# A transformer tower on one core: the engines' hand-ordered lists laid out anew, and the constant table loaded in two parts

## The chip, the cores and the metric

The kernel runs on one core of a Trainium2 chip. The metric is device time in microseconds (us) of that core; lower is better. A core has TensorE (PE in the rows, its weight loads PEld), VectorE (DVE), ScalarE (ACT), GpSimd (POOL) and SyncE (SP), which here only issues loads. Each engine runs its own program in order; an instruction that waits for a semaphore holds everything behind it on that engine.

## The reference

128 images of 3 x 64 x 64 are cut into 16 patches each (16 x 16 x 3 = 768 numbers), embedded to 192, and a class token is put ahead: 17 tokens an image. Two layers follow.

```
h0 = patches @ W.T + b, class token first                     # 17 x 192 per image
layer 0: h1 = h0 + attention(layernorm(h0))                   # 12 heads of 64; lowest scores dropped, softmax
         h2 = h1 + quantised gated feed-forward(h1)           # 8-bit rows, ternary weights, hidden 512
layer 1: h3 = h2 + linear attention(h2)                       # 12 heads of 16, causal, each head normalised,
                                                              # gate from tanh and a cosine
         out = h3 + layernorm-ed feed-forward(h3)             # hidden 128
```

## The kernel before

Seven images (119 rows, `ROWS`) are a group; 18 full groups and one of two images (34 rows) make 19. Each group goes through five chains of short instructions: patches and embedding (banks `E0`, `E1`), softmax attention (`A0`, `A1`), the quantised feed-forward (`M0`, `M1`), linear attention (`L0`, `L1`, called `bank_lin`), and the last feed-forward. The groups are staggered: in one step of the loop the newest group is embedded while the one before does its scores, the next its probabilities, and so on, six deep (`DEPTH`).

The order of the work on each engine is written out by hand as three lists of (group, piece): `fill` for steps 0 to 7 with absolute groups, `steady` for the ten steps 8 to 17 (a hardware loop over five pairs of steps; the number is how many groups behind the newest), and `drain` for the rest. `program` (line 379) runs them. Pieces on TensorE begin with `t_`, on VectorE `v_`, on ScalarE `a_`, on GpSimd `p_`. All dependences are semaphores, counted by group; so a list changes what stands behind what, never what is computed.

The pieces that matter here, with their lines. `v_sq_sum` (1088) gives the sum of squares of each head, `p_rstd_h` (622; instructions at 521 and 522) raises it to the power -1/2, `v_att1` (1092) multiplies, `t_att1` (1960) transposes it (helper `turn`, line 1554, records all transposes), `a_att1_T` copies it out. `t_down` (1873) needs `int_outT` from `a_out_T` and gives `v_h2` (1018) its input. `t_dots` (1761) gives the scores that `v_pack` (831) packs; `t_dots1` needs the packs 0 and 1. `t_embed` (1669) needs both halves of `patchT`. `v_shifted` (892), `v_feat_q`, `v_feat_k` (1052) and `v_hidT` (1041) end VectorE's list of a step; `t_params`, `t_lin_first` (1934) stand behind them on TensorE. `v_quant_in` (974) leads to ScalarE's `a_int_in`, TensorE's `t_int_in`, `t_gate`, `t_up`; then `v_gated` (983), `v_product` (990), GpSimd's `p_scaled` (551). `v_v1` (1061) and the three `v_causal` (masking products, `weightsT`, line 916) are what `t_num` (the numerators, line 1948) waits for; `t_num_turn` and `v_centred` lead on to the next `v_sq_sum`.

`zero_products` (1559) multiplies zeros into an unused bank: work for TensorE with no result, put in where it would idle. At the start TensorE multiplies 12 of them, waits for the constants (`ld_const`) and the first weights (`ld_tok`), transposes `w_tok_raw`, multiplies the start rows (1583), and enters its list. `late_setup` (358), called `wait_late` in the lists, waits for the setup's last pieces: `ready` and six loads, two of which SP issues only after VectorE's `setup_biases`.

The constant table (128 x 642) holds the identity (columns 0 to 127), the mask factors, the token kinds, the block and causal masks and two parity columns.

## Time and profile before

| | us |
|---|---|
| median of 3 runs (644.97 to 650.62) | 645.59 |
| the profiled execution, its time | 645.34 |
| its span, first to last instruction | 643.4 |
| TensorE busy | 577.2 |
| VectorE busy | 455.9 |
| ScalarE busy | 317.7 |
| GpSimd busy | 305.1 |
| mean granted clock of TensorE | 0.962 |

A granted clock of 1.00 is 2.4 GHz, 0.50 is 1.2 GHz. The page of the profile gives busy times and the costliest groups of instructions; the trace behind it can be asked who waited for whom, what ran in order of time, and how busy each engine was in a stretch. A waiting time in square brackets in a row of the order of time is idle time of that engine just ahead of the instruction, with what ended it. Start times are from the start of the span.

### The profile page before, as it was taken

How to read it: one execution, taken by the hardware profiler on the slowest of the kernel's cores; microseconds unless marked ns; L12 is line 12 of the kernel's file. 1: busy time of each engine (PE TensorE's matmuls, PEld its weight loads, DVE VectorE, ACT ScalarE, POOL GpSimd, SP SyncE). 2: the span in 40 equal slices, each digit the busy share in tenths (PEclk: the TensorE clock that was granted, in tenths of full speed). 3: DMA queues.
4: the chain of work that ended last, by engine and by line, in shares of the span. 5: the costliest groups of instructions: out<-in, count | busy, mean ns of one | idle time of the engine just before them, and what ended most of it. 6: DMA issues, size and time to landing. Idle time of an engine off the chain costs nothing. (4 is left out here: it accounts for less than half of the span.)

```text
span 643.4 us, 15871 instructions
## 1 busy us (share of the span) xinstructions
PE 577.2 (90%) x5229; PEld 468.1 (73%) x5229; DVE 455.9 (71%) x2101; ACT 317.7 (49%) x849; POOL 305.1 (47%) x788
## 2 busy tenths in 40 slices
PE   7999998989998989889897979797989899988985
PEld 4677877878887877778786868786877777764542
DVE  0587686778868577768695969586868677877743
ACT  2253755628371727273746465454646373725410
POOL 1011155455553546363646465555545454656564
PEclk7999999989996989898999999899989999979999
DMA  9721000000000000000000000000000000000000
GB/s 227 180 63 45 2 23 5 21 2 28 23 9 5 24 7 23 7 21 6 21 13 14 27 0 27 0 27 0 12 0 6 0 7 1 3 2 13 7 1 13
DMA packets 11062, 14.69 MB, mean 23 GB/s; under 512 B 2160, under 2 KB 8657, under 8 KB 11017
## 3 DMA queue, kind: packets, MB, share of 16 engines
q1 hardware_dynamic: 8712, 12.44, 7.3%
q10 hardware_dynamic: 2304, 1.67, 0.9%
q8 instruction: 25, 0.41, 0.3%
q14 instruction: 21, 0.16, 0.1%
HBM read 12.44 MB, written 1.67 MB: 22 GB/s over the span
## 5 line engine op out<-in xcount | busy, mean ns | idle before, releaser
L521 POOL TENSOR_TENSOR spread<-moments,gain_eps 119x1 f32<-119x1 f32 x57 | 10.9, 191 | 104.1 <-DVE moments L801 104.1
L522 POOL TENSOR_TENSOR rstd<-spread,minus_half 119x1 f32<-119x1 f32 (+1 forms) x95 | 55.4, 583 | 7.5
L1729 PEld LDWEIGHTS bank_embed<-norm0T,w_qkv 128*128 128x128 f32 x456 | 55.9, 194 | 3.7 <-ACT norm0T L1328 1.0
L1729 PE MATMUL bank_embed<-norm0T,w_qkv 128*128 128x119 f32 (+1 forms) x456 | 58.0, 278 | 0.0
L565 POOL TENSOR_TENSOR feat_k<-feat_qk,consts 128x238 f32<-128x238 f32 (+1 forms) x38 | 21.9, 597 | 63.3 <-DVE feat_qk L1052 63.3
L1673 PE MATMUL bank_embed<-w_tok,patchT 128*119 128x192 f32 (+1 forms) x228 | 45.6, 354 | 0.0
L1302 ACT COPY norms2T<-bank_lin 96x476 f32<-96x476 f32 (+1 forms) x19 | 10.2, 537 | 69.7 <-PE bank_lin L1554 69.7
L522 POOL TENSOR_TENSOR rstd_h<-spread_h,minus_half 119x12 f32<-119x12 f32 x19 | 43.3, 2279 | 1.5
L1673 PEld LDWEIGHTS bank_embed<-w_tok,patchT 128*119 128x119 f32 (+1 forms) x228 | 39.5, 196 | 3.1 <-issue 1.3
L1346 ACT COPY qkT<-bank_embed 128x357 f32<-128x357 f32 (+1 forms) x76 | 32.0, 445 | 18.5 <-PE bank_embed L1738 18.5
L916 DVE TENSOR_TENSOR weightsT<-bank_lin,consts 119x476 f32<-119x476 f32 (+1 forms) x57 | 34.7, 626 | 9.1 <-PE bank_lin L1934 8.8
L1832 PE MATMUL bank_att<-w_o,att0T 128*119 128x192 f32 (+1 forms) x228 | 40.9, 328 | 0.0
L831 DVE TENSOR_REDUCE scores<-bank_att 119x51 f32<-119x357 f32 (+1 forms) x76 | 36.1, 499 | 5.7 <-PE bank_att L1784 5.4
L1910 PEld LDWEIGHTS bank_lin<-norms2T,w_qkv 97*128 97x128 f32 (+1 forms) x304 | 38.1, 200 | 2.0 <-ACT norms2T L1302 1.6
L1910 PE MATMUL bank_lin<-norms2T,w_qkv 97*128 97x119 f32 (+3 forms) x304 | 39.4, 285 | 0.0
L551 POOL TENSOR_TENSOR scaled<-product,g_out 119x512 f32<-119x512 f32 x19 | 24.4, 1282 | 31.3 <-DVE product L990 31.2
L1832 PEld LDWEIGHTS bank_att<-w_o,att0T 128*119 128x119 f32 (+1 forms) x228 | 35.6, 179 | 0.8 <-ACT att0T L1374 0.2
L1554 PE MATMUL bank_lin<-consts,att 119*96 119x119 f32 (+1 forms) x38 | 8.7, 316 | 30.6 <-DVE att L1092 30.6
L1361 ACT ACTIVATE wide<-probs,consts 119x68 f32<-119x68 f32 x133 | 35.1, 346 | 0.2 <-DVE probs L907 0.2
L1738 PE MATMUL bank_embed<-norm0T,w_qkv_rest 64*128 64x119 f32 (+1 forms) x456 | 35.1, 286 | 0.0
L871 DVE MATCH_REPLACE8 kept<-top,scores 119x20 f32<-119x20 f32 x228 | 34.5, 165 | 0.0
L1328 ACT COPY norm0T<-bank_embed 128x238 f32<-128x238 f32 (+1 forms) x19 | 6.6, 349 | 56.1 <-PE bank_embed L1554 56.1
(255 smaller groups left out, 1629.7 us busy)
## 6 DMA issues: line engine op xcount, KB each, us to landing
strips<-x SPq DMA_DIRECT2D x18, 336.0 KB
out<-result ACTq DMA_DIRECT2D x18, 89.2 KB
w_qkv<-L_attn_w_qkv SPq DMA_DIRECT2D x2, 576.0 KB, 7.9
w_in_raw<-L_ffn_w_in SPq DMA_DIRECT2D x1, 768.0 KB, 12.0
w_tok_raw<-L_tok_W SPq DMA_DIRECT2D x1, 576.0 KB
w_qkv_rest<-L_attn_w_qkv SPq DMA_DIRECT2D x2, 288.0 KB, 10.0
w_o<-L_attn_w_out SPq DMA_DIRECT2D x1, 576.0 KB
w_qkv_raw<-L_attn_Wqkv SPq DMA_DIRECT2D x1, 432.0 KB
```

Of the source, the lines that this page charges most:

```text
L522: pool.tensor_tensor(rstd_out, spread, minus_half[0:ROWS, 0:spread.shape[1]], ALU.pow) \
L551: pool.tensor_tensor(scaled[:, :], product[:, :], g_out[:, :], ALU.mult).then_inc(S["scaled"], 1)
L831: dve.tensor_reduce(scores[0:r, place:place + 3, TOKENS - 1::-1], parts(src, 3)[0:r, :, 0:r].rearrange("p h (b j) -> p h j b", j=TOKENS), ...
L871: last = dve.match_replace(kept[:, h, :], top[:, h, :], scores[:, h, :], BIG)
L916: dve.tensor_tensor(dst[0:r, :, 0:r], src[0:r, :, 0:r], mask[0:r, 0:r].unsqueeze(1).to_broadcast([r, 4, r]), ALU.mult).then_inc(ready_sem, 1)
L1346: act.copy(qkT[:, p, QTILES * n + 3 * s:QTILES * n + 3 * s + 3, 0:r], parts((E0, E1)[s], 3)[:, :, 0:r]) \
L1361: last = act.activation(wide[:, 8:12, b], probs[:, 8:12, :], ACT.Copy, scale=block_mask[:, b * TOKENS:b * TOKENS + 1])
L1673: last = pe.matmul(E0[0:r, 0:EMBED], patchT[:, k, 0:r], w_tok[:, k, :], start=k == 0, stop=k == CHUNKS - 1)
L1729: pe.matmul(parts((E0, E1)[s], 3)[:, j, 0:r], w_qkv0[:, tile * 128:(tile + 1) * 128], norm0T[:, s, 0:r], start=j == 0, stop=False, skip_gr ...
L1738: last = pe.matmul(parts((E0, E1)[s], 3)[:, j, 0:r], w_qkv0_rest[rows, n, j * 128:(j + 1) * 128], norm0T[rows, 1 - s, 0:r], start=False, s ...
L1832: last = pe.matmul(A1[0:r, 0:EMBED], att0T[:, t, 0:r], w_o0[:, t, :], start=t == 0, stop=t == QTILES - 1)
L1910: last = pe.matmul(parts(L1, 4)[:, j, 0:r], w_qkv1[0:rows, k, first:first + 128], norms2T[0:rows, 2 + k, 0:r], start=k == 0, stop=k == 1)
```

## The change

All twelve lists are laid out anew: `fill`, `steady` and `drain` of TensorE, VectorE, ScalarE and GpSimd. Every piece is still there once per group. The loads and waits at the start are changed as well:

```diff
-            load(ld_const, consts[:, :], table)
+            load(ld_tok, consts[:, 0:128], table[:, 0:128])
             load(ld_tok, w_tok_raw[:, :, :], a["L0_tok_W"].rearrange("(k p) n -> p k n", k=2))
             load(ld_tok, start_rows[0:1, :], row(a["L0_tok_b"]))
             load(ld_tok, start_rows[1:2, :], a["cls_tok"].rearrange("a b n -> (a b) n"))
             load_strips(0, 0)
+            load(ld_const, consts[:, 128:C_WIDTH], table[:, 128:C_WIDTH])
...
             dve.wait_ge(ld_const, 16)
+            dve.wait_ge(ld_tok, 64)
...
-            multiply_zeros(L1, 12)
-            pe.wait_ge(ld_const, 16)
-            pe.wait_ge(ld_tok, 48)
+            multiply_zeros(L1, 21)
+            pe.wait_ge(ld_tok, 64)
...
+            pe.wait_ge(ld_const, 16)
             pe.matmul(M1[0:ROWS, 0:EMBED], token_kind, start_rows[:, :], start=True, stop=True).then_inc(setup_pe, 1)
```

The `steady` lists, TensorE's whole and of the others the stretches that the prediction speaks of:

```diff
 # TensorE
-                (4, t_params), (5, t_hid1), (4, t_lin_first), (2, t_probs1), (3, t_int_in), (5, t_out4), (2, t_probs0), (4, t_lin_rest),
-                (3, t_gate), (1, t_k_main), (3, t_up), (2, t_probs2), (1, t_k_rest), (4, t_num), (2, t_att0_0), (2, t_att0_1),
-                (4, t_num_turn), (2, t_proj0_0), (2, t_proj0_1), (3, t_int_out), (0, t_patches1), (0, t_patches0), (4, t_att1),
-                (3, t_down), (1, t_dots0), (0, t_embed), (3, t_norms2), (1, t_dots1), (4, t_proj1), (3, t_qk1), (0, t_norm0), (3, t_hid),
-                (0, t_q_main), (4, t_norm3), (0, t_q_rest), (0, t_v0), (0, t_v1),
+                (4, t_params), (5, t_hid1), (4, t_lin_first), (3, t_int_in), (5, t_out4), (2, t_probs0), (3, t_up), (3, t_gate),
+                (1, t_k_main), (4, t_lin_rest), (2, t_probs2), (2, t_probs1), (1, t_k_rest), (4, t_num), (2, t_att0_0), (2, t_att0_1),
+                (4, t_num_turn), (2, t_proj0_0), (2, t_proj0_1), (3, t_int_out), (0, t_patches1), (0, t_patches0), (3, t_down),
+                (1, t_dots0), (0, t_embed), (4, t_att1), (3, t_norms2), (1, t_dots1), (4, t_proj1), (3, t_qk1), (0, t_norm0), (3, t_hid),
+                (0, t_q_main), (0, t_q_rest), (0, t_v0), (4, t_norm3), (0, t_v1),
 # VectorE
-                (4, v_causal1), (4, v_causal0), (5, v_out4), (4, v_causal2), (3, v_gated), (3, v_product), (4, v_v1), (3, v_umax_out),
...
-                (4, v_centred), (4, v_sq_sum), (2, v_h1), (4, v_att1), (2, v_stats1), (2, v_moments1), (2, v_u_in), (3, v_h2),
-                (3, v_stats2), (3, v_moments2), (1, v_pack1), (1, v_pack0), (3, v_norms2), (5, v_moments4), (1, v_top0), (0, v_h0),
...
-                (4, v_norm3), (1, v_drop1), (1, v_mix), (1, v_least), (3, v_feat_q), (1, v_shifted), (3, v_feat_k), (3, v_hidT),
+                (3, v_amax_in), (2, v_exp_sum), (3, v_unit_in), (3, v_quant_in), (2, v_exp_inv), (2, v_probs), (2, v_wide0),
+                (4, v_causal0), (5, v_out4), (5, v_stats4), (5, v_moments4), (2, v_wide1), (4, v_causal1), (3, v_gated), (3, v_product),
+                (4, v_v1), (4, v_causal2), (3, v_row_gain), (3, v_umax_out), (3, v_amax_out), (5, v_scaled4), (3, v_unit_out),
+                (3, v_quant_out), (4, v_num_sum), (4, v_den), (4, v_centred), (4, v_sq_sum), (2, v_h1), (2, v_stats1), (3, v_h2),
+                (3, v_stats2), (3, v_moments2), (2, v_moments1), (1, v_pack1), (1, v_pack0), (4, v_att1), (3, v_norms2), (1, v_top0),
...
+                (4, v_norm3), (1, v_drop0), (1, v_mix), (3, v_feat_q), (3, v_feat_k), (1, v_least), (3, v_hidT), (1, v_shifted),
 # ScalarE
-                (3, a_int_out), (1, a_k_0), (3, a_out_T), (0, a_patchT0), (4, a_att1_T), (0, a_patchT1), (3, a_norms_T), (0, a_norm0T),
+                (2, a_probsT1), (3, a_square), (0, a_strips), (4, a_num_T), (2, a_att0), (1, a_k_0), (2, a_att1), (3, a_big_out),
+                (3, a_int_out), (1, a_k_1), (3, a_out_T), (0, a_patchT0), (0, a_patchT1), (4, a_att1_T), (3, a_norms_T), (5, a_store),
 # GpSimd
-                (4, p_wave), (5, p_h3_beta), (4, p_terms), (1, p_h0), (4, p_series), (4, p_overlap), (3, p_scaled), (3, p_rms),
-                (4, p_centred_sq), (4, p_den_sq), (4, p_rstd_h), (2, p_rstd1), (3, p_rstd2), (5, p_rstd4), (0, p_rstd0), (4, p_rstd3),
+                (4, p_wave), (4, p_terms), (4, p_series), (4, p_overlap), (5, p_h3_beta), (3, p_scaled), (3, p_rms), (1, p_h0),
+                (4, p_den_sq), (4, p_centred_sq), (4, p_rstd_h), (3, p_rstd2), (5, p_rstd4), (2, p_rstd1), (0, p_rstd0), (4, p_rstd3),
```

In `fill` and `drain` the pieces stand in much the same order as in `steady`. `wait_late` is earlier in ScalarE's `fill` (behind `(1, a_probsT1)` instead of behind `(5, a_k_1)`), later on VectorE, TensorE and GpSimd. The zero products of TensorE's lists add up to 175 where there were 152 (without the 12, now 21, at the start); the largest group, ahead of `t_att1` of the last group of images, has 22 instead of 12.

## Rows read from the trace of the kernel before

**Rows 1.** The page, part 1: busy us (share of span) x instructions of each engine.

```profile
PE 577.2 (90%) x5229; PEld 468.1 (73%) x5229; DVE 455.9 (71%) x2101; ACT 317.7 (49%) x849; POOL 305.1 (47%) x788
```

**Rows 2.** Waits of TensorE, whole span: us in total, times, longest.

```profile
PE bank_lin L1554 <- DVE att L1092: 30.6, 16, 2.6
PE bank_lin L1948 <- DVE v L1061: 11.3, 9, 1.3
PE bank_att L1778 <- DVE scores L831: 4.5, 3, 2.3
```

**Rows 3.** First, 14th `att1` in order of time; then two steps' busy time, PEclk.

```profile
105.87 0.36 DVE L1092 TENSOR_TENSOR att<-centred,rstd_h 119x192 f32<-119x192 f32 x1 [1.04 <-POOL rstd_h L522]
...
506.00 0.36 DVE L1092 TENSOR_TENSOR att<-centred,rstd_h 119x192 f32<-119x192 f32 x1 [2.02 <-POOL rstd_h L522]
...
383.09:413.31 30.22, 26.64 (x263) 23.04 (x263) 23.23 (x108) 16.57 (x44) 16.02 (x40) 1.00 0.05 14
413.31:444.55 31.24, 27.89 (x263) 24.33 (x263) 23.47 (x109) 16.57 (x44) 15.97 (x40) 0.95 0.05 14
```

**Rows 4.** Busy time and granted clock of one us behind an `att1` wait.

```profile
415.00:416.00 1.00, 1.00 (x10) 1.00 (x12) 0.88 (x4) 0.09 (x1) 0.33 (x1) 0.50 0.00 0
```

**Rows 5.** Order of time in one step: start, us, engine, line, operation [idle before].

```profile
380.06 0.35 DVE L1088 TENSOR_REDUCE sq_sum<-centred_sq 119x12 f32<-119x192 f32 x1 [0.62 <-POOL centred_sq L619]
380.78 2.28 POOL L522 TENSOR_TENSOR rstd_h<-spread_h,minus_half 119x12 f32<-119x12 f32 x1
380.86 0.56 ACT L1302 COPY int_outT<-bank_ffn 128x476 bf16<-128x476 bf16 x1 [0.49 <-PE bank_ffn L1554]
383.09 0.36 DVE L1092 TENSOR_TENSOR att<-centred,rstd_h 119x192 f32<-119x192 f32 x1 [2.02 <-POOL rstd_h L522]
384.34 0.41 DVE L1018 SCALAR_TENSOR_TENSOR h<-bank_ffn,unit_out,h 119x192 f32<-119x192 f32 x1
386.73 0.67 DVE L1033 TENSOR_SCALAR norms<-h,moments,rstd 119x192 f32<-119x192 f32 x2 [0.48 <-POOL rstd L522]
395.80 0.36 DVE L892 TENSOR_TENSOR shifted<-mixed,least 119x204 f32<-119x204 f32 x1
398.09 1.09 PE L1934 MATMUL bank_lin<-feat_qk,feat_k 32*119 32x119 f32 x16
404.53 1.27 POOL L551 TENSOR_TENSOR scaled<-product,g_out 119x512 f32<-119x512 f32 x1 [0.56 <-DVE product L990]
404.58 1.43 DVE L1061 SCALAR_TENSOR_TENSOR v<-tanh_int,v_raw 119x192 f32<-119x192 f32 x1
406.16 0.82 PE L1948 MATMUL bank_lin<-weightsT,v 119*32 119x119 f32 x24 [1.26 <-DVE v L1061]
```

**Rows 6.** Lines 1061 and 916: ns min/median/max, first and last start, forms.

```profile
L1061 DVE SCALAR_TENSOR_TENSOR v<-tanh_int,v_raw x19: 340/1409/1479, 96.5 to 626.2; 119x192 f32<-119x192 f32 x19
L916 DVE TENSOR_TENSOR weightsT<-bank_lin,consts x57: 280/642/655, 92.6 to 626.0; 119x476 f32<-119x476 f32 x54, 34x136 f32<-34x136 f32 x3
```

**Rows 7.** The start: zero products, first transposes, first patches; DMA issue of the constants.

```profile
1.20 4.09 PE L1559 MATMUL bank_lin<-zeros 128*128 128x512 bf16 x12 [1.20 <-DVE zeros L686]
7.73 2.35 PE L1554 MATMUL bank_embed<-consts,w_tok_raw 96*128 96x96 f32 x12 [2.44 <-DMA start_rows<-cls_tok]
13.04 1.29 PE L1554 MATMUL bank_embed<-consts,patches 84*128 84x84 f32 x8
...
consts<-constants SPq DMA_DIRECT2D x1, 321.0 KB, 3.4
```

**Rows 8.** Order of time in the drain, TensorE, last group of images.

```profile
627.76 2.75 PE L1559 MATMUL bank_att<-zeros 128*128 128x512 bf16 x12
632.87 0.28 PE L1554 MATMUL bank_lin<-consts,att 34*96 34x34 f32 x2 [2.35 <-DVE att L1092]
```

**Rows 9.** One step of the fill: a matmul's wait; then busy time, PEclk 0.50.

```profile
196.95 0.36 PE L1778 MATMUL bank_att<-mask_factors 64*119 64x357 bf16 x2 [1.86 <-DVE scores L831]
...
201.00:203.00 2.00, 2.00 (x10) 2.00 (x10) 1.58 (x7) 0.00 (x0) 0.00 (x1) 0.50 0.00 0
```

More of the change, by code:

```diff
@@ L2049, in _ @@
[L2049 removed]
+                (0, t_embed), (0, zero_products(E1, 11)), (0, t_norm0), (0, zero_products(E0, 2)), (0, t_v_first), (0, t_q_main),
+                (0, t_q_rest), (0, zero_products(M1, 4)), (0, t_k_main), (0, t_k_rest), (0, zero_products(M1, 4)),
+                (0, once(setup_sums_of_weights)), (0, zero_products(M1, 2)), (0, t_dots0), (1, t_patches1), (1, t_patches0),
@@ new lines, in _ @@
+                (1, t_proj0_1), (3, t_patches1), (0, t_int_out), (2, t_dots0), (0, t_down), (3, t_embed), (2, t_dots1), (0, t_norms2),
+                (3, once(setup_b2o)), (0, zero_products(E1, 1)), (0, t_hid), (0, t_qk1), (3, t_norm0), (0, t_params), (2, once(wait_late)),
+                (3, t_v0), (3, t_v1), (1, t_int_in), (3, t_q_main), (3, t_q_rest), (1, t_gate), (0, t_lin_first), (2, t_probs0),
+                (3, t_k_main), (1, t_up), (3, t_k_rest), (0, t_lin_rest), (2, t_probs1), (2, t_probs2), (0, t_num), (2, t_att0_0),
@@ new lines, in _ @@
+                (15, t_down), (17, t_dots0), (18, t_embed), (14, zero_products(E1, 2)), (14, t_att1), (17, t_dots1), (15, t_norms2),
+                (14, t_proj1), (15, t_qk1), (18, t_norm0), (18, zero_products(A0, 1)), (18, t_v0), (14, t_norm3), (15, t_hid),
+                (14, t_hid1), (18, t_q_main), (15, t_params), (14, t_out4), (18, t_q_rest), (18, t_v1), (16, t_int_in), (15, t_lin_first),
+                (16, t_gate), (18, t_k_main), (16, t_up), (15, t_lin_rest), (18, t_k_rest), (17, t_probs0), (17, t_probs1), (15, t_num),
```

397 lines of the change are left out of this document (192 added, 205 removed).

## The prediction

> **What bounds the kernel now.** I read the page's busy times first: TensorE works 577.2 us of the 643.4 us span, so about 66 us of its idle time are all that an order of the work can win, beside what the clock takes [rows 1]. The waits of TensorE say where they lie: 30.6 us in 16 waits for `att1` (line 1092), 11.3 us in 9 waits for `v1` (line 1061), and 4.5 us in 3 waits for `scores` [rows 2]. The first two repeat in every step of the loop. From the `att1` of group 0 to that of group 13 pass 13 steps and 400.13 us, 30.78 us a step [rows 3]. Two steps side by side show the second loss: with the same count of matmuls one lasts 30.22 us with the granted clock at 1.00 and 26.64 us of TensorE work, the next 31.24 us at 0.95 and 27.89 us of work [rows 3]. The clock stands at 0.50, the 1.2 GHz level, just behind the second step's wait for `att1` [rows 4].
>
> The third view is the order of time inside the full-clock step [rows 5]. I measure from the end of `sq_sum` at 380.41. GpSimd raises `rstd_h` from 380.78 to 383.06 (2.28 us). VectorE's next instruction in its list but one is `v_att1`, so it idles 2.02 us, and TensorE idles with it. `h2`, ready for long (its transposed input `int_outT` was copied at 381.42), starts at 384.34. From there VectorE is dense to `shifted` (395.80), with one idle of 0.48 us before `norms2`; then come `lin_first` on TensorE (398.09), `scaled` on GpSimd (404.53, released by VectorE's `product`), `v1` (404.58 to 406.01), the numerators (406.16), and the next `sq_sum` 30.22 us after the first. This is a ring through four engines: shortening TensorE's own wait gives nothing unless VectorE arrives earlier too.
>
> **The change, part by part.**
>
> *Step of the loop.* (a) `t_att1` now stands behind `t_down`, `t_dots0` and `t_embed`, `v_att1` behind `h1`, `stats1`, `h2`, `stats2`, both moments and the packs 1 and 0; `a_patchT1` no longer stands behind `a_att1_T`, so both halves of `patchT` are there for the embedding. `t_down` can start at about 381.5, when `int_outT` is copied, take the 0.5 us of a small matmul group, and `h2` starts near 382.05 instead of 384.34: 2.3 us earlier. `rstd_h` is then covered by the work above: VectorE reaches `att1` near 384.0, 0.9 us after it is ready. (b) From `h2` to `shifted` VectorE took 11.46 us. Five short instructions come in (`att1`, `u_in`, `moments1`, `feat_k`, `hidT`), two leave (`moments4`, `scaled4`): three more at the 0.36 us of `att1`, 1.1 us; the 0.48 us idle is filled. 12.1 us, so `shifted` starts near 394.15, 1.65 us earlier, with `feat_k` and `hidT` (0.6 us) already done, which before stood behind it. The quantisation and TensorE's `lin_first` thus come 2.3 us earlier. (c) `t_int_in`, `t_up` and `t_gate` move ahead; `t_int_in` stands directly behind `t_lin_first` and I expect about 0.35 us of waiting there, paid out of TensorE's slack before the numerators, so nothing on the ring. (d) On GpSimd `p_h0` and `p_h3_beta` leave the chain that ends in `overlap`; it ends earlier, but `v1` has to wait for `product` as before: nothing. (e) `v_causal2` moves from before `gated` to behind `v1`, and the numerators need it. That puts one more masking instruction, 0.64 us [rows 6], between `v1` and `t_num`: +0.65. Nothing hides it. (f) The tail from the numerators to `sq_sum` keeps its order apart from `a_strips` (ahead of `a_num_T` now), hidden by the two attention groups.
>
> Sum of a step: 30.22 - 2.3 + 0.65 = 28.57 us. TensorE then idles some 1.9 us a step, in gaps no longer than the 1.26 us that it has now before the numerators. (g) The clock: it fell only behind gaps near 2 us, so I take it as held; the average step goes from 30.78 to 28.57. Over the 13 steps: -28.7 us. The lists ahead of and behind the loop have the same new order, so I count the fill's steps with the loop's and the first step of the drain as one more, -2.0.
>
> *Bounds of a step.* Below: all 26.64 us of work and only the 1.26 us wait left, 27.9. Above: nothing won on the ring, 30.22 plus 0.65. I take 28.57, since the row of `int_outT` shows `h2`'s input there 2.9 us before `h2` ran.
>
> *The start.* The transposes of `w_tok` start at 7.73, released by the last of the first weights; 321 KB of constants had gone ahead, in 3.4 us from issue to landing [rows 7]. Now only the identity's 64 KB do, 257 KB less; at the 94 KB/us of those 321 KB in 3.4 us (which holds a latency too, so this is an upper end) that is at most 2.7 us, and at least 0. TensorE's zero products go from 12 to 21. The first 12 took 4.09 us [rows 7]; nine more at the 0.23 us of those near the end [rows 8] end at about 7.4. So the weights are no longer what is late: the transposes start near 7.4, but at the clock that the zero products have warmed, where before they ran at half. They and the five zero products behind them then need some 2.3 us less, and the patches come near 10.8 instead of 13.04 [rows 7]. The rest of the constants is queued behind the strips; the start matmul, the bf16 identity and the mask factors wait for it. It has 1.6 us of transposes as cover; without it, each us late is a us lost. Against this, ScalarE's `wait_late` moves ahead by more than a group, to where the two small bias rows are just being reloaded by SP's queue: 0 to 2 us once, I take 0.5. Its neighbours (`setup_ready`, GpSimd's and VectorE's `wait_late`, the pieces of weight rounding) cost nothing: TensorE has work of groups 0 and 1 over them. Start: -2.3 + 0.5 = -1.8, bounds -2.8 and +2.
>
> *The drain.* Zero products over the whole list go from 152 to 175. At 0.23 us the 23 more are 5.3 us if none is hidden. Ten stand ahead of `att1` of the last group: the 12 there end at 630.51, that `att1` arrives at 632.87 [rows 8], so 22 just fit. For the other 13 I count 3.0 us. Against it the longest `scores` wait, 2.3 us [rows 2], which lies in the drain, should go, and with it a fall of the clock like the one of 1.0 us that separates the two steps of [rows 3]: -0.3, bounds -4 and +5.
>
> Total: -28.7 - 2.0 - 1.8 - 0.3 = -32.8. From the profiled execution's own time, 645.34 us (1.94 above its span and 0.25 below the median of the three runs, so no correction), that gives 612.5, rounded to **612 us**.
>
> *A rule weighed.* `v1` takes 1409 ns in the median and 340 ns at best [rows 6]; in the step shown it starts 0.05 us after GpSimd's `scaled` and ends 0.2 us behind it [rows 5]. The Trainium skill (GPSIMD Engine Reference, Key points) says that GpSimd shares its SBUF interfaces with VectorE and contends with instructions that have two SBUF inputs. The trace agrees for this pair; it is what makes the rival below possible.
>
> **The rivals.**
> 1. *As worked out*: 612 us. For it: every piece of the wait has ready work behind it. Chance 0.60.
> 2. *One more collision on the ring.* The new order puts other pairs side by side (`h3_beta` close before `scaled`, `wide1` beside the `overlap` chain). One collision costs 1409 - 340 = 1.07 us; once a step over 13 steps, 14 us: 626 us. Against it: that chain has slack to `product`. Chance 0.19. The sharing that the Trainium skill's GPSIMD Engine Reference (Key points) states would make it so.
> 3. *The wait only changes its name.* One step of the fill shows it already: there `t_embed` stood ahead of `t_att1`, but VectorE was still held by `att1`, and TensorE lost 1.86 us at `scores` instead, the clock then falling to 0.50 [rows 9]. If in the loop the ring stays at 30.22 and only the clock is mended, 13 x 0.56 = 7 us and the start's 1.8 remain: 636 us. Against it: this time the packs stand ahead of `v_att1` too. Chance 0.08.
> 4. *Slower.* The place is VectorE between `h2` and `shifted`. If the stretch grows by the instructions brought in and by idle time, so that `shifted` comes no earlier than 395.80, then `causal2` (+0.65) and the early `t_int_in` (which stops `t_out4`, `t_probs0` and all behind, about +0.2) are pure cost, and TensorE's gaps stay long enough to lose the clock: 31.6 us a step, +0.8 x 13 = 10.4 us: 656 us, the start's gain being used up by the drain's zero products. It decides once 1.5 of the 2.3 us are lost there. Chance 0.08.
> 5. *More than forecast*: `causal2` or `v1` finds a free slot and the step reaches 27.9 or less: 600 us and below. Chance 0.05.
>
> **How the numbers follow.** A measurement of this kernel tells about 1% (6.5 us) from no change. Rival 4 is slower; a tenth of rivals 2 and 3 and of my error in the drain ends within 1%, 0.04; the rest is faster: faster 0.88, same 0.04, slower 0.08. The range runs from 600 (step at its lower bound, 13 x 0.67 = 9 us, with a good drain) to 636 (rival 3) and leaves out rival 4, the draw and most of rival 5, 0.17.
>
> **What would show it.** `att1` on TensorE no longer among its longest waits, and those for `v1` replaced by `weightsT` (`causal2`) at about 1.3 us each; 28.6 us between two `att1` of the loop; granted clock 1.00 in every step; `h2` running before `att1` on VectorE; patches near 10.8 us. I am wrong if the step is 30 us or more, if waits for `scores` or `norms2` of 1 us turn up in each step, if the wait at `t_int_in` exceeds 1 us, or if the clock still falls every second step.

## The result, and the profile after

The changed kernel takes 592.75 us (median of four, 590.95 to 593.97) against 648.11 (644.97 to 651.63) for the kernel before in the same comparison: ratio 0.9142, 95% interval 0.9076 to 0.9208. Forecast were 612 us and a range of 600 to 636: the kernel got faster, as forecast, but the gain is 55 us where 33 were worked out, and the time lies 7 us below the range. The profiled execution took 593.97 us, with a span of 592.1 and a mean granted clock of 0.988.

The page, part 1, and TensorE's longest waits (us in total, times, longest), as in [rows 1, 2]:

```profile
PE 574.2 (97%) x5261; PEld 455.6 (77%) x5261; DVE 437.8 (74%) x2101; ACT 314.6 (53%) x849; POOL 304.9 (51%) x788
...
PE bank_att L1780 <- DVE h L940: 1.9, 5, 0.7
PE bank_att L1690 <- DMA w_qkv_rest<-L_attn_w_qkv: 1.9, 1, 1.9
PE bank_lin L1936 <- issue: 1.3, 1, 1.3
```

The waits for `att1` and `v1` are no longer in the list, and none took their place: TensorE is busy 97% of the span. Two steps side by side, which answer to [rows 3] (start and end of the step and its length, busy time and number of instructions of PE, PEld, DVE, ACT and POOL, granted clock, share and GB/s of the DMA):

```profile
325.65:352.40 26.75, 26.67 (x264) 22.81 (x263) 22.07 (x109) 16.21 (x44) 15.82 (x41) 1.00 0.06 16
352.40:379.59 27.19, 27.07 (x266) 23.01 (x265) 22.12 (x109) 16.31 (x44) 16.20 (x41) 1.00 0.06 16
```

The length of the step and TensorE's work in it differ by 0.1 us: the loop is bound by TensorE, at full clock. The forecast step was 28.57 us, bound by the ring. The order of time in the second of them, against [rows 5] (lines moved by one or two):

```profile
348.61 0.35 DVE L1090 TENSOR_REDUCE sq_sum<-centred_sq 119x12 f32<-119x192 f32 x1 [0.62 <-POOL centred_sq L620]
350.42 0.42 DVE L1020 SCALAR_TENSOR_TENSOR h<-bank_ffn,unit_out,h 119x192 f32<-119x192 f32 x1 [0.74 <-PE bank_ffn L1879]
352.40 0.35 DVE L1094 TENSOR_TENSOR att<-centred,rstd_h 119x192 f32<-119x192 f32 x1
361.91 0.51 DVE L894 TENSOR_TENSOR shifted<-mixed,least 119x204 f32<-119x204 f32 x1
364.05 0.21 DVE L976 TENSOR_SCALAR quant_in<-ainv_in,rstd 119x1 f32<-119x1 f32 x1
369.16 0.69 DVE L992 TENSOR_TENSOR product<-bank_ffn,gated 119x512 f32<-119x512 f32 x1
369.36 0.30 ACT L1455 ACTIVATE tanh_int<-tanh_over,temp 119x12 f32<-119x12 f32 x1
369.77 0.35 DVE L1063 SCALAR_TENSOR_TENSOR v<-tanh_int,v_raw 119x192 f32<-119x192 f32 x1
369.93 1.33 POOL L552 TENSOR_TENSOR scaled<-product,g_out 119x512 f32<-119x512 f32 x1 [0.46 <-DVE product L992]
370.03 0.65 DVE L918 TENSOR_TENSOR weightsT<-bank_lin,consts 119x476 f32<-119x476 f32 x1
371.23 0.82 PE L1950 MATMUL bank_lin<-weightsT,v 119*32 119x119 f32 x24
375.69 0.35 DVE L1090 TENSOR_REDUCE sq_sum<-centred_sq 119x12 f32<-119x192 f32 x1 [0.62 <-POOL centred_sq L620]
```

`h2` now runs ahead of `att1`, which waits for nothing. And `v1` starts 0.16 us ahead of `scaled` and takes 0.35 us, where it started 0.05 us behind it and took 1.43. All 19 `v1` together (ns min/median/max) were 340/1409/1479 in [rows 6]:

```profile
L1063 DVE SCALAR_TENSOR_TENSOR v<-tanh_int,v_raw x19: 316/348/1467, 95.7 to 574.5; 119x192 f32<-119x192 f32 x19
```

**The miss as a sum.** From the first `att1` to the 14th the trace after has 354.35 us:

```profile
105.91 0.34 DVE L1094 TENSOR_TENSOR att<-centred,rstd_h 119x192 f32<-119x192 f32 x1
...
460.26 0.35 DVE L1094 TENSOR_TENSOR att<-centred,rstd_h 119x192 f32<-119x192 f32 x1
```

| stretch | before | after | gain | forecast |
|---|---|---|---|---|
| start to first `att1` | 105.87 | 105.91 | 0.0 | 1.8 |
| 13 steps | 400.13 | 354.35 | 45.8 | 28.7 |
| 14th `att1` to the end of the span | 137.4 | 131.8 | 5.6 | 2.3 |

Nearly the whole miss, 17.1 of 18.6 us, lies in the 13 steps, and there in the loop itself: the four steps of the fill gained 9.7 us (forecast 8.8), the nine behind them 36.1 (forecast 19.9). Inside the step the same events, from one `sq_sum` to the next (before in the full-clock step, `quant_in` at 397.90 and `product` at 403.76 there):

| | before | forecast | after |
|---|---|---|---|
| `sq_sum` to `quant_in` | 17.84 | 15.54 | 15.44 |
| `quant_in` to `product` | 5.86 | 5.86 | 5.11 |
| `product` to the numerators | 2.40 | 3.05 | 2.07 |
| numerators to `sq_sum` | 4.12 | 4.12 | 4.46 |
| sum | 30.22 | 28.57 | 27.08 |

The term that the prediction worked out longest, steps (a) and (b), came out to 0.1 us. The miss is in the two terms costed at nothing, (c) and (d), which shorten the step by 0.75 and 1.29 us; (e) and the tail, (f), are some 0.3 us longer each than forecast and give part of it back.

### The profile page after: what moved, and what is told of

Read it like the earlier page. It is cut to its first block, busy times and chain, and to the rows that moved or that the text cites. A ratio compares the mean times of both kernels' runs of the same rounds, so it can differ in the third digit from the quotient of the medians.

```text
span 592.1 us, 15935 instructions
## 1 busy us (share of the span) xinstructions
PE 574.2 (97%) x5261; PEld 455.6 (77%) x5261; DVE 437.8 (74%) x2101; ACT 314.6 (53%) x849; POOL 304.9 (51%) x788
## 4 chain that ended last, share of the span: by engine, by line
PE 84%; DVE 7%; issue 2%; DMA 2%; ACT 2%; POOL 2%; SPq 1%; POOLq 0%; DVEq 0%; ACTq 0%
PE bank_embed L1731 8%; PE bank_att L1834 6%; PE bank_lin L1912 6%; PE bank_embed L1740 5%; PE bank_lin L1936 5%; PE bank_embed L1675 5%; PE bank_att L1556 5%; PE bank_att L1823 4%; PE bank_lin L1556 4%; PE bank_att L1690 4%; PE bank_att L1561 4%; PE bank_att L1786 3%; PE bank_ffn L1556 3%; PE bank_embed L1556 2%; PE bank_lin L1950 2%; PE bank_lin L1975 2%
## 5 line engine op out<-in xcount | busy, mean ns | idle before, releaser
L566 POOL TENSOR_TENSOR feat_k<-feat_qk,consts 128x238 f32<-128x238 f32 (+1 forms) x38 | 23.6, 642 | 38.5 <-DVE feat_qk L1054 38.5
L1675 PE MATMUL bank_embed<-w_tok,patchT 128*119 128x192 f32 (+1 forms) x228 | 41.7, 333 | 0.0
L1348 ACT COPY qkT<-bank_embed 128x357 f32<-128x357 f32 (+1 forms) x76 | 32.9, 443 | 12.8 <-PE bank_embed L1740 12.1
L1304 ACT COPY att1T<-bank_lin 96x238 f32<-96x238 f32 (+1 forms) x19 | 6.6, 346 | 59.2 <-PE bank_lin L1556 59.2
L1675 PEld LDWEIGHTS bank_embed<-w_tok,patchT 128*119 128x119 f32 (+1 forms) x228 | 35.6, 179 | 3.0 <-ACT patchT L1322 0.9
L1912 PEld LDWEIGHTS bank_lin<-norms2T,w_qkv 97*128 97x128 f32 (+1 forms) x304 | 36.0, 191 | 2.3 <-ACT norms2T L1304 2.2
L1912 PE MATMUL bank_lin<-norms2T,w_qkv 97*128 97x119 f32 (+3 forms) x304 | 37.5, 277 | 0.0
L873 DVE MATCH_REPLACE8 kept<-top,scores 119x20 f32<-119x20 f32 x228 | 34.4, 165 | 0.0
L1936 PE MATMUL bank_lin<-feat_qk,feat_k 32*119 32x119 f32 (+1 forms) x456 | 33.0, 277 | 1.3 <-issue 1.3
```

The lines of the kernel that those rows point to most:

```text
L873: last = dve.match_replace(kept[:, h, :], top[:, h, :], scores[:, h, :], BIG)
L1675: last = pe.matmul(E0[0:r, 0:EMBED], patchT[:, k, 0:r], w_tok[:, k, :], start=k == 0, stop=k == CHUNKS - 1)
L1912: last = pe.matmul(parts(L1, 4)[:, j, 0:r], w_qkv1[0:rows, k, first:first + 128], norms2T[0:rows, 2 + k, 0:r], start=k == 0, stop=k == 1)
L1936: last = pe.matmul(lin[0:r, lin_column[slot]:lin_column[slot] + r], feat_k[32 * q:32 * q + 32, odd, t, 0:r], feat_qk[32 * q:32 * q + 32, t ...
```

## The experiments

Each carries one part alone, or takes one away. The ring is the prediction's: the chain through four engines from one `sq_sum` to the next. The theory: two losses were removed from the ring, the wait for `att1` and the slow `v1`, and the second went because `tanh_int` comes earlier, so that `v1` starts ahead of `scaled`. The first rival: only the wait for `att1` counted. For each kernel the table has the nine steps from the fifth to the 14th `att1` (no fill, no drain in them), from the profiled execution, with their granted clock. The ratio is to the kernel before as timed again in the same group of runs. Its median there was 644.77 to 651.58 us, so a difference of a few us between the medians of two rows can come from the group alone; the steps agree more closely, 26.93 to 26.95 us in the six kernels that have the new loop.

| kernel | median us | ratio, 95% interval | us a step | clock |
|---|---|---|---|---|
| before | 648.11 | | 30.94 | 0.96 |
| after | 592.75 | 0.9142, 0.9076 to 0.9208 | 26.93 | 1.00 |
| b_loop | 607.18 | 0.9336, 0.9241 to 0.9432 | 26.95 | 1.00 |
| b_att | 628.92 | 0.9746, 0.9675 to 0.9816 | 28.90 | 1.00 |
| b_pool | 641.15 | 0.9876, 0.9786 to 0.9966 | 29.96 | 0.96 |
| b_att_pool | 613.51 | 0.9504, 0.9435 to 0.9572 | 27.62 | 1.00 |
| b_three | 607.41 | 0.9464, 0.9366 to 0.9562 | 26.65 | 1.00 |
| b_att_gap | 623.86 | 0.9647, 0.9466 to 0.9828 | 28.15 | 1.00 |
| b_att_pe (step of an execution of 674.98) | 656.02 | 1.0105, 1.0011 to 1.0199 | 34.30 | 0.85 |
| b_att_gate | 628.92 | 0.9636, 0.9516 to 0.9756 | 28.24 | 1.00 |
| b_lin_late | 623.01 | not on record | 28.04 | 1.00 |
| a_pool_back | 599.45 | 0.9320, 0.9236 to 0.9404 | 27.67 | 1.00 |
| a_att_back | 625.91 | 0.9730, 0.9632 to 0.9828 | 30.42 | 0.95 |
| a_start_back | 593.09 | 0.9121, 0.9077 to 0.9164 | 26.94 | 1.00 |
| a_fill_back | 600.43 | 0.9240, 0.9170 to 0.9309 | 26.95 | 1.00 |
| a_drain_back | 602.44 | 0.9276, 0.9225 to 0.9327 | 26.95 | 1.00 |
| a_nozero | 605.44 | 0.9342, 0.9273 to 0.9411 | 26.95 | 1.00 |
| a_three | 588.48 | 0.9060, 0.9001 to 0.9120 | 26.67 | 1.00 |

A name with b_ is the kernel before with something of the change in it, one with a_ the kernel after with something taken back.

### The loop's lists alone (b_loop)

The four `steady` lists of after in the kernel before; nothing else.

> The kernel before with the changed lists of the loop alone (fill, drain and start as before). The step after the change lasted 27.26 us against 30.78 before, 3.52 us less in each of 13 steps, 45.8 us. Theory: nearly the whole gain lies in the loop's order, so 648 - 46 = 602 us, with 26.7 to 27.3 us between two att1 and no wait of TensorE over 0.5 us in the loop. Rival: the loop only runs so well because the new fill hands it over in the right phase; with the old fill it keeps a stall a step, 28.5 us or more, 618 us or more.

By the medians of its group, 39.5 of the 55 us are the loop's. The step is the same as after the change; TensorE's waits for `v1` are gone. But just ahead of the loop, with the old fill, one step lasts 34.8 us at a granted clock of 0.85, where after the change it has 27.4 us:

```profile
193.29:228.11 34.82, 31.58 (x267) 27.82 (x266) 25.35 (x118) 16.48 (x44) 17.56 (x43) 0.85 0.05 14
```

Not all of that is the fill's order. Behind the same wait of 1.86 us for `scores` the clock stayed at 1.00 in the traces of b_att and a_fill_back, which have the old fill too, and this step lasted 30.1 and 30.6 us. So the order is worth some 3 us here, and a fall of the clock that does not come in every execution another 4.

### One cause or two (b_att, b_pool, b_att_pool)

```diff
 # b_att, steady. TensorE:
-(4, t_att1), (3, t_down), (1, t_dots0), (0, t_embed),
+(3, t_down), (1, t_dots0), (0, t_embed), (4, t_att1),
 # VectorE: (4, v_att1) from behind (2, v_h1) to behind (1, v_pack0)
 # ScalarE: (0, a_patchT1) ahead of (4, a_att1_T)
 # b_pool, steady, GpSimd:
-(4, p_wave), (5, p_h3_beta), (4, p_terms), (1, p_h0), (4, p_series), (4, p_overlap), (3, p_scaled), (3, p_rms),
+(4, p_wave), (4, p_terms), (4, p_series), (4, p_overlap), (5, p_h3_beta), (3, p_scaled), (3, p_rms), (1, p_h0),
 # b_att_pool: both
```

> The kernel before; in the loop alone the att1 products, their mask and their rounding stand behind the embedding and the packs, as after the change, and nothing else is moved. GpSimd's h3_beta and h0 stay where they were, ahead of overlap. Theory (two causes): this takes the 2.0 us wait off the ring, but v1 still starts behind scaled and lasts some 1.4 us, so the step is 27.9 to 28.6 us, the total 648 - 13 x 2.5 = 615 us (612 to 620). Rival (one cause): the wait for att1 was all; the collision of v1 with scaled goes by itself once the phase has moved: 27.3 us a step, 603 us.

> The kernel before; in the loop alone GpSimd's h3_beta stands behind overlap and h0 behind the rms alone, so the chain that ends in overlap and releases tanh_int is some 1 us shorter. Nothing else is moved. Theory (two causes): tanh_int comes before product, v1 starts ahead of scaled and lasts some 0.35 us instead of 1.4: 1.07 us less on the ring, 30.78 - 1.07 = 29.7 us a step, 634 us, with TensorE's wait for att1 as before or longer. Rival (one cause): what GpSimd does ahead of overlap is of no account, 648 us within 3.

> Both of the two edits above in the kernel before. Theory (two causes): TensorE becomes the bound, 26.7 to 27.5 us a step as after the change, 648 - 13 x 3.4 = 604 us. Rival (one cause): the same as with the move of att1 alone. Rival (a third move, such as the other masking instruction causal2 behind v1, is needed too): between 608 and 615 us.

Both edits shorten the step, as the theory says and the first rival denies: 28.90 us with the move of `att1` alone, 27.62 with both. But no step is as short as the theory had it (27.9 to 28.6 and 26.7 to 27.5), the medians lie 9 us above its figures, and with both edits 613.51 us falls where the rival of a third move had put it, 608 to 615; b_three below has that third move. Order of time at `v1` in the kernel with `att1` moved, and then in the one with both:

```profile
328.36 0.69 DVE L990 TENSOR_TENSOR product<-bank_ffn,gated 119x512 f32<-119x512 f32 x1 [0.45 <-PE bank_ffn L1950]
328.89 0.30 ACT L1508 ACTIVATE tanh_int<-tanh_over,temp 119x12 f32<-119x12 f32 x1
329.13 1.27 POOL L551 TENSOR_TENSOR scaled<-product,g_out 119x512 f32<-119x512 f32 x1 [0.52 <-DVE product L990]
329.23 1.38 DVE L1061 SCALAR_TENSOR_TENSOR v<-tanh_int,v_raw 119x192 f32<-119x192 f32 x1 [0.18 <-ACT tanh_int L1508]
330.76 0.82 PE L2036 MATMUL bank_lin<-weightsT,v 119*32 119x119 f32 x24 [1.25 <-DVE v L1061]
```

```profile
351.82 0.69 DVE L1004 TENSOR_TENSOR product<-bank_ffn,gated 119x512 f32<-119x512 f32 x1 [0.46 <-PE bank_ffn L1964]
352.43 0.35 DVE L1075 SCALAR_TENSOR_TENSOR v<-tanh_int,v_raw 119x192 f32<-119x192 f32 x1
352.60 1.33 POOL L551 TENSOR_TENSOR scaled<-product,g_out 119x512 f32<-119x512 f32 x1 [0.98 <-DVE product L1004]
352.93 0.82 PE L2050 MATMUL bank_lin<-weightsT,v 119*32 119x119 f32 x24
```

Here `v1` waits 0.18 us for `tanh_int` itself; that puts it 0.10 us behind `scaled` and costs 1.03 us more. With the shorter GpSimd chain there is no wait, and the numerators start 1.11 us behind `product` instead of 2.40.

The move on GpSimd alone gave 5.5 us where 14 were expected. `v1` took 0.35 us in every one of its steps there too, and two of the nine steps have the 29.0 to 29.2 us that a collision less makes of 30.22; but TensorE's wait for `att1` stayed (31.0 us in 16), and behind it the clock fell in the others: TensorE's busy time is 28.1 us in this step, 26.6 in a full-clock one.

```profile
376.09:406.36 30.27, 28.09 (x263) 24.79 (x263) 22.19 (x109) 16.72 (x44) 16.13 (x40) 0.94 0.05 14
406.36:435.37 29.01, 26.60 (x263) 23.05 (x263) 22.07 (x109) 16.74 (x44) 16.18 (x40) 1.00 0.05 15
```
By the medians the same edit is worth 5.5 us alone and 15.4 us behind the other, but only part of that difference is the loop's: it takes 0.98 us off a step alone (30.94 to 29.96) and 1.28 behind the other (28.90 to 27.62). Alone, the stretch from the 14th `att1` to the end was 5.9 us longer than before (143.4 against 137.5); why was not followed.

### Is it the order of v1 and scaled, or the shorter chain? (b_att_gap)

```diff
             def p_scaled(g, p):
                 pool.wait_ge(S["product"], g + 1)
                 after(pool, RUN["a_quant_out"], g)
+                pool.tensor_tensor(spacer[:, :], ones[0:ROWS, 0:HEADS], ones[0:ROWS, 0:HEADS], ALU.mult)
                 pool.tensor_tensor(scaled[:, :], product[:, :], g_out[:, :], ALU.mult).then_inc(S["scaled"], 1)
```

> The kernel before with the move of att1 (the step of 28.88 us, in which v1 started 0.09 us behind scaled and lasted 1.40 us), and one instruction more: a product of 119x12 ones on GpSimd, of the 0.21 us of its neighbours, between the wait for product and scaled. It computes nothing that is used. Nothing of the chain to tanh_int is shortened. Theory (which of v1 and scaled starts first decides): scaled starts 0.2 us later, v1 ahead of it and lasts 0.35 us; 27.8 us a step, 13 x 1.05 = 14 us less than the 628.9 us, 615 us. The kernel gets faster by an instruction. Rival (a shorter GpSimd chain is what helped): 629 to 632 us. Rival (v1 is slow in any overlap with scaled): the same 629 to 632.

One instruction more on GpSimd for each group, and the step is 0.75 us shorter in the mean of nine, 0.85 in the last eight. Order of time:

```profile
361.80 0.30 ACT L1510 ACTIVATE tanh_int<-tanh_over,temp 119x12 f32<-119x12 f32 x1
362.04 0.21 POOL L552 TENSOR_TENSOR spacer<-ones 119x12 f32<-119x12 f32 x1 [0.52 <-DVE product L992]
362.13 0.36 DVE L1063 SCALAR_TENSOR_TENSOR v<-tanh_int,v_raw 119x192 f32<-119x192 f32 x1 [0.17 <-ACT tanh_int L1510]
362.20 1.43 POOL L553 TENSOR_TENSOR scaled<-product,g_out 119x512 f32<-119x512 f32 x1
```

`tanh_int` comes no earlier against `product` and `v1` still waits 0.17 us for it; only `scaled` starts later. `v1` is 0.07 us ahead and takes 0.36 us, `scaled` takes 1.43 instead of 1.27. Both rivals are out: which of the two starts first decides. The Trainium skill (SBUF — State Buffer, SBUF: two separate sides) says of the port pair that VectorE and GpSimd share that whichever starts first has it for the whole instruction and the other blocks. The traces agree: 0.35 us ahead, 1.38 to 1.48 when 0.0 to 0.1 us behind, 0.83 when 0.65 behind, ending 0.2 us after `scaled` each time. In all 18 traces together the border is sharp. The 186 `v1` that start between 0.16 us ahead of `scaled` and 0.003 us behind it take 0.34 to 0.36 us, and `scaled` ends 1.13 to 1.17 us after them, whatever the lead; the 90 that start 0.005 to 0.66 us behind take 0.83 to 1.48 us and end 0.21 to 0.22 us after `scaled`. By the medians the total gained only 5 of the expected 14 us, and the two intervals overlap. The nine steps give 6.8 us; in this execution the step ahead of the loop took 34.4 us, against 30.1 in that of b_att, with the fall of the clock described at b_loop.

### What the rest of the loop is worth (b_three)

The kernel with both edits, and on GpSimd, steady:

```diff
-(2, p_rstd1), (3, p_rstd2), (5, p_rstd4),
+(3, p_rstd2), (2, p_rstd1), (5, p_rstd4),
```

> The kernel before with both edits (att1 behind the packs, h3_beta and h0 out of the way; 27.62 us a step, 613.5 us), and in the loop also GpSimd's rstd1 of group 2 behind rstd2 of group 3. The step with two edits shows VectorE idle 1.18 us at norms2 for rstd2, and TensorE waits 12.1 us in 14 places for norms2. Theory (this is what the whole new loop has over the two edits, 0.65 us a step): 26.9 to 27.1 us a step, 605 us, no wait for norms2. Rival (other moves of the new lists did it, rstd1 comes too late for amax_in now): 27.6 us or more, 613 us or more.

26.65 us: VectorE's wait at `norms2` was the next stall of the ring. With both edits alone it read

```profile
334.79 0.67 DVE L1047 TENSOR_SCALAR norms<-h,moments,rstd 119x192 f32<-119x192 f32 x2 [1.18 <-POOL rstd L522]
335.59 0.61 PE L1656 MATMUL bank_lin<-consts,norms 119*96 119x119 f32 x4 [0.96 <-DVE norms L1047]
```

and with the third the idle time is 0.20 us and TensorE does not wait. Three moves in four lists make a step 0.3 us shorter than the whole new loop.

### TensorE's part of the move alone (b_att_pe)

The lists of TensorE and ScalarE of b_att, without VectorE's move.

> The kernel before; in the loop TensorE's and ScalarE's part of the move of att1 alone. On VectorE att1 stays where it was, ahead of stats1 and h2, where it waits for rstd_h. Theory (the ring leads through VectorE, so a move on TensorE alone only gives the wait another name): VectorE still idles 2 us at att1, h2 and the packs come as late as before, TensorE waits for scores or norms2 instead: 30.2 us a step or more, 643 to 648 us. Rival (TensorE's order is what counted): 629 us, as with the whole move.

The mechanism of the prediction's rival 3, made real: nothing is gained. The ratio is 1.0105 (interval 1.0011 to 1.0199), and the median lies above the 643 to 648 us expected. The trace is of the longest of five executions, 674.98 us, so its 34.30 us a step and clock of 0.85 are not typical of the median of 656.02; what waits for what can be read from it. TensorE's wait is now at `norms2`, 27.7 us in 15 places, up to 2.6 us. VectorE idles at `att1` as before and `h2` starts behind it:

```profile
323.71 0.36 DVE L1092 TENSOR_TENSOR att<-centred,rstd_h 119x192 f32<-119x192 f32 x1 [2.22 <-POOL rstd_h L522]
324.96 0.41 DVE L1018 SCALAR_TENSOR_TENSOR h<-bank_ffn,unit_out,h 119x192 f32<-119x192 f32 x1
327.36 0.67 DVE L1033 TENSOR_SCALAR norms<-h,moments,rstd 119x192 f32<-119x192 f32 x2 [0.48 <-POOL rstd L522]
```

In these steps `v1` starts level with `scaled`, 0.02 us ahead at most, and takes 0.36 us. The collision is gone here too, and it does not help while VectorE waits at `att1`.

### Taking the two causes back (a_pool_back, a_att_back)

```diff
 # a_pool_back, steady, GpSimd: (5, p_h3_beta) behind (4, p_wave), (1, p_h0) behind (4, p_terms)
 # a_att_back, steady: (4, t_att1) ahead of (3, t_down), (4, v_att1) behind (2, v_h1), (4, a_att1_T) ahead of (0, a_patchT1)
```

> The kernel after the change; in the loop alone GpSimd's h3_beta and h0 go back ahead of overlap, as before. Theory (the order in which v1 and scaled start decides): tanh_int comes some 1 us later, behind product, v1 starts behind scaled and lasts 1.4 us, and causal2 with its 0.65 us follows it on the path to the numerators; this is the step of 28.57 us that was forecast. 27.9 to 28.6 us a step, 604 to 614 us. Rival (TensorE's slack takes it up, the loop stays bound by TensorE's 27 us of work): 593 to 597 us.

> The kernel after the change; in the loop alone the att1 products, their mask and their rounding go back to their old places ahead of the down projection, the down projection's residual and the second half of the patches. Theory: the wait of about 2 us for att1 comes back in each step and with it a clock that falls in some of them; v1 keeps its 0.35 us. 29.2 to 30.2 us a step against 26.97, so 622 to 635 us. Rival (the ring has been shortened enough elsewhere for the wait to be covered): under 610 us.

Without the GpSimd moves the step is 27.67 us, 0.74 longer, less than the 1 to 1.6 expected, and the median is between theory and rival. `tanh_int` came so late that `v1` waits for it, 0.65 us behind `scaled`, and `causal2` does follow it on the path:

```profile
374.36 1.27 POOL L552 TENSOR_TENSOR scaled<-product,g_out 119x512 f32<-119x512 f32 x1
375.01 0.84 DVE L1077 SCALAR_TENSOR_TENSOR v<-tanh_int,v_raw 119x192 f32<-119x192 f32 x1 [0.73 <-ACT tanh_int L1469]
375.77 0.64 DVE L932 TENSOR_TENSOR weightsT<-bank_lin,consts 119x476 f32<-119x476 f32 x1
376.47 0.82 PE L1964 MATMUL bank_lin<-weightsT,v 119*32 119x119 f32 x24 [0.55 <-DVE weightsT L932]
```

`product` (373.59) to the numerators is 2.88 us here and 3.06 in every other step; the forecast had 3.05. The rest of the gap to 28.57 is the earlier `product`. Taking `att1` back costs 33 us by the medians, 3.5 us a step, and brings TensorE's wait for it (20.5 us in 10 places) and a clock of 0.95 back: this is the larger cause, with what it does to the clock.

### What brought product nearer (b_att_gate, b_lin_late)

```diff
 # b_att_gate: b_att, TensorE, steady
-(4, t_lin_first), (2, t_probs1), (3, t_int_in), (5, t_out4), (2, t_probs0), (4, t_lin_rest), (3, t_gate), (1, t_k_main), (3, t_up),
+(4, t_lin_first), (3, t_int_in), (2, t_probs1), (5, t_out4), (2, t_probs0), (4, t_lin_rest), (3, t_up), (3, t_gate), (1, t_k_main),
 # b_lin_late: b_att_pool, TensorE, steady
+(4, t_lin_first), (3, t_int_in), (5, t_out4), (2, t_probs0), (3, t_up), (3, t_gate), (1, t_k_main), (4, t_lin_rest), (2, t_probs2), (2, t_probs1),
 # and VectorE: (4, v_causal2) behind (4, v_v1), (2, v_wide0) ahead of (2, v_wide1)
```

> The kernel before with the move of att1 (28.90 us a step, bound by the ring), and in the loop TensorE's transposes of int_in ahead of those of the probabilities, and the up projection directly ahead of the gate instead of 1.4 us of other products behind it. Theory (the second term that was sized wrong): from quant_in to product passed 5.84 us in that kernel and 5.11 after the whole change; product no longer waits its 0.45 us for the up projection and int_in is transposed some 0.1 to 0.3 us sooner, so 28.2 to 28.5 us a step and 0.4 to 0.7 us less between quant_in and product. Over nine steps 4 to 6 us: 623 to 625 us. Rival (these moves give the ring nothing, as the forecast had it, and the up projection ahead of the gate makes gated late by its 0.6 us): 28.9 us a step or more, 629 us or more.

> The kernel before with the two edits (27.62 us a step; from quant_in to product 5.85 us, from product to the numerators 1.11), and TensorE's whole stretch behind lin_first as after the change: the transposes of int_in first, one group of probabilities, the up projection, the gate, and only then the rest of the linear products and the other two groups; VectorE's causal2, which needs those linear products, behind v1, and wide0 ahead of wide1. Theory (what brought product 0.75 us nearer is that one group of probabilities and the rest of the linear products no longer stand ahead of the gate, paid with causal2 behind v1): quant_in to product 5.1 to 5.2 us, product to numerators about 2.07 as after the change, so 27.62 - 0.75 + 0.96 = 27.8 us a step, no gain from the pair of moves: 612 to 617 us. Rival (the 0.75 us come from elsewhere in the lists): quant_in to product 5.6 us or more.

The first moved the wrong pieces: from `quant_in` (385.98) to `product` passed 6.32 us, 0.5 more than in b_att, since `gated` now waits 1.06 us for `tanh_gate`; the rival was right on that. The step is 0.65 us shorter all the same (the two medians are equal, from different groups), for a reason that neither expected: `product`, and `scaled` behind it, come late enough for `v1` to be first.

```profile
392.30 0.69 DVE L990 TENSOR_TENSOR product<-bank_ffn,gated 119x512 f32<-119x512 f32 x1
392.91 0.35 DVE L1061 SCALAR_TENSOR_TENSOR v<-tanh_int,v_raw 119x192 f32<-119x192 f32 x1
393.08 1.35 POOL L551 TENSOR_TENSOR scaled<-product,g_out 119x512 f32<-119x512 f32 x1 [1.01 <-DVE product L990]
```

The second: `quant_in` (409.20) to `product` (414.53) is 5.33 us against 5.85 in b_att_pool, so 0.5 of the 0.75 us come with this set of moves, and by b_att_gate it is not the early `t_int_in` and `t_up` that bring them but one group of probabilities and the rest of the linear products, which now stand behind the gate; the other 0.2 are open. It is paid for: `product` to the numerators is 2.09 us instead of 1.11, as `causal2` now stands there. On the whole these moves made the step longer, 28.04 against 27.62, and the median, 623.01, is above the 612 to 617 expected.

### Start, fill, drain, zero products (a_start_back, a_fill_back, a_drain_back, a_nozero)

The kernel after with the old loads, waits and 12 zero products at the start; with the four old `fill` lists; with the four old `drain` lists; and with all `zero_products` taken out of TensorE's `drain` (they compute nothing).

> The kernel after the change with the old start alone: the constants loaded whole ahead of the first weights, 12 zero products instead of 21, the start matmul not waiting for the rest of the constants. Theory: the first numerators came 0.9 us earlier after the change, so the old start costs 1 to 2 us: 594 to 595 us, with the patches at about 13 us instead of 10.6. Rival (the wait of TensorE for the second load of attention weights, 1.9 us after the change, takes the gain up): 593 us, no difference.

> The kernel after the change with the old lists of the fill. Theory: between the first and the fifth att1 passed 122.9 us in the kernel before with the new loop, 111.9 after the whole change; the 10.9 us are the fill's order, so 604 us. Rival (those 11 us come from the phase in which the new start sets the fill, not from its lists): under 597 us.

> The kernel after the change with the old lists of the drain. From the att1 of group 13 to the end passed 134.7 us in the kernel before with the new loop, 131.8 after the whole change. Theory: the new drain is worth those 2.9 us, 596 us. Rival (the added zero products cost as much as the order gives back): 591 to 594 us.

> The kernel after the change without the zero products in the drain, which compute nothing. Theory (they fill time in which TensorE would idle and hold its clock): the clock falls to 0.50 behind the waits of the last groups and the drain gets 1 to 4 us longer: 594 to 597 us. Rival (some of them stand in the path, as was counted at 3 us in the forecast): 588 to 592 us.

*Start*: 0.3 us between the medians, inside their spread. The patches came at 10.56 us, forecast 10.8 (11.89 with the old start in this trace). At the next load TensorE then waits 1.87 us for `w_qkv_rest`, and of the 1.33 us 0.96 are left behind it (19.63 against 20.59) and 0.7 at the first `att1` (105.91 against 106.60). None of this is clear of the scatter between executions: in traces that share the new start and fill this wait is 0 (a_nozero) to 1.87 us, the patches come at 10.54 to 11.84 (10.24 to 13.04 with the old start), and the first `att1` at 103.8 to 106.8.

```profile
1.20 6.25 PE L1561 MATMUL bank_lin<-zeros 128*128 128x512 bf16 x21 [1.20 <-DVE zeros L687]
10.56 0.75 PE L1556 MATMUL bank_embed<-consts,patches 84*128 84x84 f32 x8
...
19.63 1.52 PE L1690 MATMUL bank_att<-w_qkv,norm0T 128*119 128x384 f32 x4 [1.87 <-DMA w_qkv_rest<-L_attn_w_qkv]
```

*Fill*: 7.7 us by the medians, 6.0 by the traces in the four steps of the fill (117.9 against 111.9), between theory and rival. *Drain*: 9.7 us by the medians, where the trace shows 3.1 (134.9 us from the 14th `att1` to the end, 131.8 after); both theory and rival missed that, and what the rest is stays open: the profiled execution, 598.32, was the shortest of four, at a clock of 0.99 against 0.976 in the others. *Zero products*: without them 12.7 us more, of which the trace has 12.6 behind the 14th `att1` (144.4 against 131.8). That is far over the theory's 1 to 4, and the rival, that they cost more than they give, is out. In the drain without them, then with them (the columns are those of [rows 3]):

```profile
500.00:530.00 30.00, 25.85 (x269) 20.04 (x269) 24.36 (x113) 18.15 (x54) 20.78 (x56) 0.89 0.01 2
530.00:560.00 30.00, 24.70 (x137) 17.58 (x132) 12.95 (x46) 8.72 (x22) 12.65 (x36) 0.56 0.01 4
```

```profile
500.00:530.00 30.00, 28.87 (x269) 21.07 (x268) 23.41 (x114) 17.23 (x53) 20.23 (x59) 0.94 0.01 3
530.00:560.00 30.00, 29.67 (x240) 17.31 (x240) 18.26 (x66) 12.13 (x32) 19.87 (x48) 1.00 0.02 5
```

### A version that beats both (a_three)

The kernel after, with the `steady` lists of b_three.

> The kernel after the change, with the loop's lists of the kernel before and three edits in them alone (att1 behind the packs, h3_beta and h0 out of the way of overlap, rstd1 behind rstd2). In the kernel before these made a step of 26.65 us, against 26.96 us with the new lists. Theory: 13 x 0.31 = 4 us less than after the change, 589 us, and a chip with nothing left to win in the loop, its TensorE busy 26.59 of 26.65 us. Rival (the step of 26.65 us came from the hand-over of the old fill, or the new drain wants the new loop): 592 us or more.

588.48 us, 4.3 less than after the change by the medians, 0.9060 of before (0.9001 to 0.9120) beside 0.9142 (0.9076 to 0.9208); the two intervals overlap, the step does not: 26.67 against 26.93. TensorE idles for 0.06 us in it:

```profile
298.91:325.55 26.64, 26.58 (x265) 23.07 (x264) 22.04 (x109) 16.73 (x44) 16.13 (x41) 1.00 0.06 16
```

## Why the prediction was right and wrong

- **The ring, steps (a) and (b): the mechanism right, the sum in part luck.** `h2` starts 1.81 us behind `sq_sum`, forecast 1.99; `quant_in` at 15.44, forecast 15.54. But the move of `att1` alone brings `quant_in` only to 16.50 (b_att): VectorE then idles 1.1 to 1.2 us at `norms2` for `rstd`. The last 1.0 us came with GpSimd's `rstd2` ahead of `rstd1` (15.51 in b_three), a move that the prediction gave no part in it; it took the idle time at `norms2` as filled by the work moved in. And inside the stretch two errors cancel: from `h2` to `shifted` passed 11.49 us, forecast 12.1, and from there to `quant_in` 2.14, where the forecast left 1.45, since VectorE waits 0.89 us for ScalarE's `expd` at `exp_sum`. That VectorE must move with TensorE was right: b_att_pe gains nothing.
- **(c), `t_int_in`, `t_up` and `t_gate` early, "nothing on the ring": wrong by 0.75 us.** `product` comes that much nearer to `quant_in`. I had followed `t_int_in` and not asked what was taken out from ahead of the gate; b_lin_late shows 0.5 of it.
- **(d), "`v1` has to wait for `product` as before: nothing": the step that failed.** I had both the price (1.07 us) and the row in which `v1` starts 0.05 us behind `scaled`, and used them only for a rival in which something gets slower. `product` did end before `v1` could start, but not by much: it ended at 404.45, `tanh_int` at 404.55, and `scaled` started at 404.53, `v1` at 404.58. A tenth of a microsecond decided, and the two pieces that leave GpSimd's chain bring `tanh_int` forward by more than that. b_pool, b_att_pool and b_att_gap show it.
- **(e), `causal2` behind `v1`, +0.65, "Nothing hides it": the cost is real, and right for the case that was forecast.** With `v1` held up it is 0.48 to 0.66 us (a_pool_back, 2.88 to 3.06 against 2.40); without the collision it is 0.98 (b_lin_late, 2.09 against 1.11). From `product` to the numerators (d) takes 1.29 off (2.40 to 1.11), (e) puts 0.96 on: 2.07 instead of 3.05.
- **(f), the tail from the numerators to `sq_sum`, unchanged: wrong by 0.34 us** (4.46 against 4.12). It is 4.12 again in a_pool_back; the cause was not followed.
- **The lower bound of 27.9 us fell with (d)**: it kept the 1.26 us wait for `v1`. Without that wait only the 26.64 us of work were a bound; the step after has 26.93.
- **(g), the clock: right in the loop.** 1.00 through it once the gaps near 2 us are gone (also in b_att, which keeps gaps of 1.26 and 0.9 us), 0.95 when they come back. In the drain it does not hold that the clock falls only behind such gaps: after the change it stood at 0.50 from 506.1 for 3.4 us and from 564.1 for 10.2 us, and TensorE has no idle time over 0.7 us from 190 us to the end.
- **The start: wrong.** The patches came to 0.2 us as forecast; the wait for the next weights behind them I had not looked for. These weights land at 17.1 to 20.1 us in the seven traces with the new start and at 14.3 to 16.9 in the eleven with the old. In both orders the same bytes are loaded ahead of them, in one load more now, so why they land that much later is open. 1.8 us forecast, none at the first `att1` against before, 0.3 by the medians.
- **The drain: sized low.** The zero products were counted at 3.0 us of cost; without them the kernel is 12.7 us slower. From the 14th `att1` to the end 5.6 us were won where 2.3 were forecast.
- **Rival 2** (one more collision) had its mechanism right and its sign wrong. Rival 5, with a chance of 0.05, is what happened; "`v1` finds a free slot" stood in it without a number.

## What to carry to other kernels

Where a row shows two instructions of VectorE and GpSimd side by side and one of them four times its shortest time, look which starts first and by how much: if the margin is a tenth of a microsecond, any change upstream of either decides it, and both signs belong in the forecast. When one wait on a ring is removed, ask of every other link what it would be without its own stall before calling the sum a bound. And a move that frees one engine must be made on all engines of the ring: on TensorE and ScalarE alone it gained nothing here.
